# A fused Flamingo block on one core: the QKV products are scheduled two slots earlier, and the splitting of a weight moves between ScalarE, GpSimd and VectorE

## What is computed

```python
ln_out = _ln(hidden_states, ln_w, ln_b)
q  = _ln(_fp8_linear_pertensor(ln_out, wq, wq_scale, q_in_scale).reshape(b, s, g, hpg, d), qln_w, qln_b)
k  = _ln(_fp8_linear_pertensor(ln_out, wk, ...), kln_w, kln_b)
v  = _fp8_linear_pertensor(ln_out, wv, ...)
core = _gqa(q, k, v)                      # softmax(q k / sqrt(d)) v
qx = _ln(_fp8_linear_pertensor(ln_out, wqx, ...), qxln_w, qxln_b)
kx, vx = jnp.split(jnp.einsum('bsi,oi->bso', cond, w_kv_x), 2, axis=-1)
xout = _gqa(qx, _ln(kx, kxln_w, kxln_b), vx)
catq = _div_clamp_fp8(jnp.concatenate([core, xout], axis=-1), proj_smooth)
x = x + jnp.tanh(g_xattn[0]) * jnp.einsum('bsi,oi->bso', catq, wproj) * (proj_in_scale * proj_w_scale)
...
h = bitlinear(_layernorm(x), w_gate_up)   # ternary weights, activations quantized per row
a, b = jnp.split(h, 2, axis=-1)
x = x + jnp.tanh(g_ffn[0]) * bitlinear(jax.nn.silu(a) * b, w_down)
```

## Time and profile before

| | |
|---|---|
| median of 3 runs | 1846.1 us (1844.93 to 1848.54) |
| the profiled execution | 1844.93 us, its span 1843.1 us |
| granted TensorE clock, mean over the span | 0.965 |
| PE, DVE, ACT, POOL busy | 88%, 84%, 74%, 60% of the span |

### The profile page before, as it was taken

How to read it: one execution, slowest core, us unless ns; L and a number is a source line. 1 busy time by engine, 2 the same in 40 slices (tenths; PEclk the granted TensorE clock), 3 DMA queues, 4 the chain that set the end, 5 groups by cost and what they waited for, 6 DMA issues and landing times.

```text
span 1843.1 us, 35164 instructions
## 1 busy us (share of the span) xinstructions
PE 1625.3 (88%) x11147; PEld 1007.0 (55%) x11164; DVE 1543.7 (84%) x3419; ACT 1358.0 (74%) x3383; POOL 1099.5 (60%) x1421
## 2 busy tenths in 40 slices
PE   1368888788999999999999888999999978999995
PEld 1355555455666665666666555666666524444442
DVE  7568899999897899988788999999988857777774
ACT  6468999778989998999997788989988842222222
POOL 3577888777786787888676667767777620000000
PEclk8689999989999999999999999999999989999997
DMA  3257889779999999999898988999998976322200
GB/s 102 95 147 168 183 194 209 167 163 205 226 247 192 206 236 193 207 227 252 187 220 178 224 192 202 233 219 225 226 223 172 206 180 207 92 74 77 69 18 17
DMA packets 669596, 325.48 MB, mean 177 GB/s; under 512 B 552288, under 2 KB 595424, under 8 KB 669152
## 3 DMA queue, kind: packets, MB, share of 16 engines
q1 hardware_dynamic: 669408, 323.17, 78.1%
HBM read 140.61 MB, written 48.23 MB: 102 GB/s over the span
## 4 chain that ended last, share of the span: by engine, by line
PE 43%; DVE 26%; ACT 11%; POOL 8%; issue 7%; DMA 4%; SPq 1%; ACTq 0%; DVEq 0%; POOLq 0%
PE psum L699 8%; PE psum L654 7%; PE psum L687 7%; PE psum L741 6%; PE psum L716 6%; DVE pp L981 5%; DVE nmx L971 5%; PE psum L661 3%; PE psum L758 3%; DMA pt<-pp 3%; ACT pp L1321 2%; PE psum L674 2%; ACT psum L1310 2%; DVE xh L954 1%; ACT raw L1241 1%
## 5 line engine op out<-in xcount | busy, mean ns | idle before, releaser
L687 PE MATMUL psum<-qk 128*128 128x512 f16 x1536 | 423.3, 385 | 28.6 <-DVE pp L981 22.5
L699 PE MATMUL psum<-pt,vv 128*128 128x512 f16 x1536 | 398.7, 383 | 37.2 <-ACT cy L1329 22.0
L654 PE MATMUL psum<-wbt,xqt 128*128 128x256 f16 (+1 forms) x4096 | 406.7, 249 | 15.9 <-DVE xqt L898 11.4
L1310 ACT ACTIVATE psum<-psum,nmx 128x512 f32<-128x512 f32 x512 | 349.1, 682 | 76.6 <-DVE nmx L971 75.4
L654 PEld LDWEIGHTS psum<-wbt,xqt 128*128 128x128 f16 x4096 | 329.5, 99 | 125.4 <-DVE xqt L898 11.6
L981 DVE SCALAR_TENSOR_TENSOR pp<-psum,prs,pp 128x512 f16<-128x512 f32 x512 | 379.3, 741 | 2.6 <-ACT pp L1321 2.4
L971 DVE TENSOR_REDUCE nmx<-psum 128x1 f32<-128x512 f32 x512 | 345.5, 675 | 30.7 <-PE psum L687 30.0
L1321 ACT ACTIVATE pp<-psum,prs 128x512 f16<-128x512 f32 x512 | 361.7, 706 | 6.1 <-DMA pt<-pp 5.7
L699 PEld LDWEIGHTS psum<-pt,vv 128*128 128x128 f16 x1536 | 147.4, 98 | 234.5 <-issue 47.4
L1564 POOL TENSOR_TENSOR qk<-y,qk 128x512 f16<-128x512 f32 x192 | 232.7, 1212 | 16.0
L687 PEld LDWEIGHTS psum<-qk 128*128 128x128 f16 x1536 | 143.3, 99 | 115.6 <-DVE pp L981 28.1
(11 more groups left out here) (176 smaller groups left out, 2773.0 us busy)
## 6 DMA issues: line engine op xcount, KB each, us to landing
wbt<-ws SPq DMA_DIRECT2D x192, 256.0 KB, 3.8
ws<-wbt SPq DMA_DIRECT2D x64, 256.0 KB, 4.0
catd<-cy SPq DMA_DIRECT2D x64, 256.0 KB, 3.4
raw<-in_wgu SPq DMA_DIRECT2D x64, 256.0 KB, 3.6
raw<-in_w SPq DMA_DIRECT2D x32, 384.0 KB, 3.8
wbt<-catd SPq DMA_DIRECT2D x6, 2048.0 KB, 9.9
pt<-pp SPq DMA_TRANSPOSE x512, 3.8
raw<-in_wp SPq DMA_DIRECT2D x32, 256.0 KB, 3.6
```

The lines of the kernel that those rows point to most:

```text
L654: ins = e.matmul(bank[:, o0:o0 + c1 - c0], xv[:, v, kt * 512 + tt * 128:kt * 512 + (tt + 1) * 128], wb[i][:, h, kt, c0:c1], start=kt == 0 ...
L687: ins = e.matmul(SB(n), qk[i][:, jq, u, ss], qk[i][:, jk, w, :], start=k == 0, stop=k == 2)
L699: ins = e.matmul(OB, v[:, t, u, att, :], src[:, w, t, :], start=t == 0 and k == 0, stop=t == 3 and k == 2)
L1310: e.activation(SB(n), SB(n), ACT.Exp, bias=nmx[:, k], accum_out=psm[:, k]).then_inc(s["exp"], 1)
```

## The change

- The QKV products move two slots earlier (GEMM_AT 9 to 7), with what belongs to them: the ramp begins two slots earlier (FIRST), the first weights are loaded earlier, `group_factors`, the stores of the split weights and the loads for the end move, and the reload of stored weights (`load_w`) comes one slot earlier. Part 0 now falls on t = 2, part 1 on t = 3, part 2 on t = 0, part 3 on t = 1.
- PVS becomes 1, 1, 2 and 0 units; the first head transpose of a group moves from t = 1 to t = 0.
- The four `x_turn` move by one or two slots; `scale_whole` moves one slot earlier and `weight_scales` too; `ctx_hi` and `ctx_lo` ("parts") move two slots earlier.
- A split changes engines: POOL makes the float16 copy (slot m), DVE the subtraction (slot m+1). ACT keeps the sum.
- For group 1 the first product waits for all six weight tiles, not for four.

```diff
-FIRST, PAST = -26, NSLOT + 20
+FIRST, PAST = -28, NSLOT + 20
 PVLAG = 9
-PVS = ((0,), (1, 2), (3,), ())
-GEMM_AT = 9
+PVS = ((0,), (1,), (2, 3), ())
+GEMM_AT = 7
-HEADS_AT = (10, 12, 14, 16, 18, 22)
-FACTORS_AT = 6
+HEADS_AT = (9, 12, 14, 16, 18, 22)
+FACTORS_AT = 4
-RAMP_LOAD = (-27, -26, -25, -20, -20, -19)
-W0_AT = -22
+RAMP_LOAD = (-29, -28, -27, -22, -20, -19)
+W0_AT = -24
-STORE_W = 10
+STORE_W = 8
-WG_AT, CAT_AT, X2_AT = (444, 490), (474, 498), 507
+WG_AT, CAT_AT, X2_AT = (444, 488), (472, 496), 506
-SCALE_AT = {"sum": 303, "whole": 308, "fac": 309}
+SCALE_AT = {"sum": 303, "whole": 307, "fac": 308}
-    "turn": (19, 24, 35, 51),
+    "turn": (20, 26, 36, 52),
-    "parts": (104, 104, 104, 104),
+    "parts": (102, 102, 102, 102),
...
-                nw, j = divmod(n + 7 + 2 * SLOTS, SLOTS)
+                nw, j = divmod(n + 8 + 2 * SLOTS, SLOTS)
...
-                            q.wait_ge("w_dn", it * 6 + (6 if it > 1 else 4))
+                            q.wait_ge("w_dn", it * 6 + (6 if it else 4))
...
# DVE, job(m), a split:
+                    q.wait_ge("l_hi", JV["l_hi", m])
+                    if stored is not None:
+                        q.wait_ge(f"l_st{i}", JV[f"l_st{i}", stored])
+                        q.wait_ge("l_ab", JV["l_ab", summed])
+                    e.tensor_tensor(o.bitcast(F16)[:, 0:512], f, wps[:, j, :], ALU.subtract).then_inc(s["l_lo"], 1)
...
# ACT:
-            def job_hi(m):
-                j, i = JOBS[m][2], (K0 + m) % 2
-                q.wait_ge(f"raw_ld{i}", JV[f"raw_ld{i}", K0 + m])
-                e.activation(wps[:, j, :], raw[i][:, 0:512], ACT.Copy).then_inc(s["l_hi"], 1)
...
# POOL, job(m), a split:
-                    e.tensor_tensor(o.bitcast(F16)[:, 0:512], f, wps[:, j, :], ALU.subtract).then_inc(s["l_lo"], 1)
+                    q.wait_ge(f"raw_ld{i}", JV[f"raw_ld{i}", K0 + m])
+                    e.tensor_scalar(wps[:, j, :], raw[i][:, 0:512], 1.0, 1.0, ALU.mult, ALU.mult).then_inc(s["l_hi"], 1)
...
-                if JOB_AT.get(n - 1, -1) >= 0:
-                    job(JOB_AT[n - 1])
+                if JOB_AT.get(n, -1) >= 0:
+                    job(JOB_AT[n])
```

More of the change, by code:

```diff
@@ L998, in job @@
             def job(m):
-                if JOBS[m][0] != "tern":
+                what, src, j, _ = JOBS[m]
+                i = (K0 + m) % 2
+                f, o = raw[i][:, 0:512], raw[i][:, 512:768]
+                if what in ("sum", "scale"):
                     return
-                i = (K0 + m) % 2
-                f, ob = raw[i][:, 0:512], raw[i][:, 512:768].bitcast(BF16)[:, 0:512]
                 stored, summed = JB[m]
-                q.wait_ge("l_t1", JV["l_t1", m])
-                q.wait_ge(f"l_st{i}", JV[f"l_st{i}", stored])
-                q.wait_ge("l_ab", JV["l_ab", summed])
-                q.done(e.tensor_scalar(ob, f, MAGIC, 1.0, ALU.subtract, ALU.min))
-                e.tensor_scalar(ob, ob, -1.0, None, ALU.max).then_inc(s["l_t2"], 1)
+                if what == "tern":
+                    ob = o.bitcast(BF16)[:, 0:512]
+                    q.wait_ge("l_t1", JV["l_t1", m])
+                    q.wait_ge(f"l_st{i}", JV[f"l_st{i}", stored])
+                    q.wait_ge("l_ab", JV["l_ab", summed])
+                    q.done(e.tensor_scalar(ob, f, MAGIC, 1.0, ALU.subtract, ALU.min))
+                    e.tensor_scalar(ob, ob, -1.0, None, ALU.max).then_inc(s["l_t2"], 1)
+                else:
+                    q.wait_ge("l_hi", JV["l_hi", m])
+                    if stored is not None:
+                        q.wait_ge(f"l_st{i}", JV[f"l_st{i}", stored])
+                        q.wait_ge("l_ab", JV["l_ab", summed])
+                    e.tensor_tensor(o.bitcast(F16)[:, 0:512], f, wps[:, j, :], ALU.subtract).then_inc(s["l_lo"], 1)
             def weight_sums():
@@ L1416, in act_program @@
                     ctx_hi(b, kt)
-                if JOB_AT.get(n, -1) >= 0 and JOBS[JOB_AT[n]][0] == "split":
-                    job_hi(JOB_AT[n])
                 for at in (n, n - 2):
@@ L1580, in job @@
                 i = (K0 + m) % 2
-                f, o = raw[i][:, 0:512], raw[i][:, 512:768]
                 if what == "split":
-                    stored, summed = JB[m]
-                    q.wait_ge("l_hi", JV["l_hi", m])
-                    if stored is not None:
-                        q.wait_ge(f"l_st{i}", JV[f"l_st{i}", stored])
-                        q.wait_ge("l_ab", JV["l_ab", summed])
-                    e.tensor_tensor(o.bitcast(F16)[:, 0:512], f, wps[:, j, :], ALU.subtract).then_inc(s["l_lo"], 1)
+                    q.wait_ge(f"raw_ld{i}", JV[f"raw_ld{i}", K0 + m])
+                    e.tensor_scalar(wps[:, j, :], raw[i][:, 0:512], 1.0, 1.0, ALU.mult, ALU.mult).then_inc(s["l_hi"], 1)
             q.wait_ge("pre_v", 1)
```

## The result

| | before | after |
|---|---|---|
| median | 1845.0 us (1843.05 to 1848.54) | 1863.4 us (1856.64 to 1868.18) |
| ratio, 95% interval | | 1.0092 [1.0077, 1.0107] |
| profiled execution, its span | 1844.9, 1843.1 us | 1860.7, 1858.9 us |

A forecast was written before the change was run, and what follows sets the result against it. DVE and ACT handing over in each slot were taken to bound slots 0 to 368, PE slots 368 to 488; terms -2 + 3 - 3 - 5 + 4 + 0 - 2 = -5 us gave 1840 profiled, 1841 median, range 1828 to 1857.

The forecast's parts named there:

- What bounds the kernel: Whole kernel: PE bounds slots 440 to 488 and the stretch ahead; DVE and ACT set the pace in 0 to 368.
- The splits: Slots 96 to 304: DVE gains 32 subtractions of 0.85 us, a quarter felt; +4 us, bounds -6 and +30.
- the splits make DVE the bound: Rival, DVE in slots 93 to 306: splits cost +25 us in place of +4, giving 1862 us; chance 0.12.
- PE's four slots: PE's work spread more evenly, longest slot 3.25 to 3.05 us, `stats_a` waits less: -2 us, between -9.6 and +5.
- the new company: DVE's and ACT's four slots, 96 to 368: same work, other instructions sharing a slot; +3 us, between -5 and +15.
- the new company hurts: Rival: ACT's longer slot t = 2 is not made up, +15 us in place of +3, giving 1853 us; chance 0.13.
- The x transposes: Two slots between head and x transpose would end 8.1 us of waits in slots 0 to 96: -3, between -8 and +6.
- no change: Rival: the removed stalls were of an engine that was ahead, so 1846 us, within 0.2%; chance 0.27.
- scale_whole: Slot 308: PE's 3.16 us stall and some 3.2 of slow clock go, 1.5 is new: -5 us, bounds -7 and +1.
- The ramp: Ahead of slot 0: two slots longer but the same weight chain, PE idle there anyway; 0 us, between -1 and +3.
- The end: Slots 486 and 487 lose their products, 1.7 us of PE work moved ahead: -2 us, bounds -3 and 0.
- The signs that I had named as wrong: Slots 96 to 304 over 550 us; DVE split over 1.2 or waiting 10 us; ACT's waits moved; slot 0 over 3 us later.

The follow-up runs named there:

- e2: Kernel before with only the splits changed (POOL copies, DVE subtracts one slot later, ACT sums): 1854.8 us, ratio 1.0041.
- e1: The whole change but with the splits left as in the kernel before: 1846.8 us, ratio 1.0012 to before.
- e8: e1 with ACT's `norm_b` written one slot later, at t = 3 instead of t = 2: 1891.7 us, ratio 1.0242 to before.
- e14: e1 with the products one slot earlier than before instead of two (GEMM_AT 8), and what belongs to them: 1944.3 us, ratio 1.0541 to before.
- e6: Kernel before with only PVS changed to 1, 1, 2, 0 units: 1839.6 us, ratio 0.9964.
- e15: e1 with ACT's four context copies in slot 103 instead of 102: 1843.5 us, ratio 0.9990 to before.
- e16: The whole changed kernel with the context copies in slot 103 instead of 102: 1861.6 us, ratio 1.0077 to before.
- e10: e1 with the first head transpose back in slot 10 and the x transposes in slots 19, 24, 35, 52: 1848.4 us, ratio 1.0013 to before.
- e9: e1 with the output chain behind ACT's copy (clip, subtraction, DVE's steps, store) two slots later: 1864.2 us, ratio 1.0085 to before.
- e3: Kernel before with only `scale_whole` and `weight_scales` one slot earlier and the last x transpose at slot 52: 1842.5 us, ratio 0.9987.
- e4: Kernel before with only the splits' subtraction moved from POOL to DVE, ACT still copying: 1848.8 us, ratio 1.0019.
- e5: e2 with DVE's subtraction replaced by a shorter instruction with one SBUF input that writes zeros: 1850.9 us, ratio 1.0021 to before.

## Why the prediction was wrong, term by term

- **What bounds the kernel.** Right: DVE and ACT handing over in each slot set slots 96 to 304, and PE's stretches hardly moved (-0.3 and -1.3 us). Its boundaries were 2 to 3 us late (the stretch is 543.5 us long, not 546), which changes no term by more than that.
- **The splits: +4 predicted, +12.7 measured in e2.** The rival "the splits make DVE the bound" had +25. This is the first step that failed, and it is one of size: the duration on DVE was 1.08 us in the mean (34.65 busy for 32; 0.98 in e2), not 0.85, and not a quarter of it was felt but two fifths (12.7 of e2's 31.5 us). I named the wait for POOL and its 2.09 us example and gave it no term; it is 9.3 us in 11 waits and breeds the block behind it. Felt per split were 0.4 us (12.7 / 32), near the 0.5 at which I had let the rival decide. My -3 for ACT and POOL was not seen: ACT's 10 us less of work turned into waiting for DVE (39.0).
- **PE's four slots -2 and the new company +3: together +1, measured +11.4 in e1**, which for the stretch holds both, with the moved heads, x transposes and context copies. This is the second failed step, and what is seen of it fits the rival "the new company hurts": t = 2 became the longest slot (2.94 us for 2.64) and t = 3 grew too (2.64 for 2.39), while t = 0 and t = 1 gave back only 0.34 together. So the surplus that I let be made up by the next slot was not made up. Half a line of the term was right: L940 no longer waits. But I valued company by adding up lists for each slot; e8 and e14 show how little such a list can tell: one instruction pair a slot later costs 16 us, all products a slot off 57. In e8 what the list leaves out is seen, when a bank comes free; what it is in e1 stays open.
- **PVS** was predicted inside those -2. Alone it is worth 6.6 us (e6).
- **The context copies** ("parts", 104 to 102) had no term. At the two places where they stand, e15 gives back under 1 us and e16 2.4.
- **The x transposes: -3 predicted, no gain found in e10**, which takes back the distance but not the whole wait. The waits vanished as predicted, L626 is down from the earlier trace rows to the line below; the rival "no change" had said that these were stalls of an engine that was ahead. The same PE gained waits of 7.8 us for heads behind x and 6.3 for weights in slots 0 to 96. That stretch did gain 4 to 5 us, by something that e10 leaves in place and e9 undoes; what it is stays open. A candidate that the prediction didn't name: PE's largest wait there, 12.4 us for POOL at L600, is down to 2.0 after and 1.8 in e10. Its lines before and after stand first; no run tests it.

```profile
PE psum L600 <- POOL spread L1467: 12.4, 5, 4.7
PE psum L600 <- POOL spread L1469: 2.0, 4, 0.9
PE psum L626 <- ACT y L1312: 1.4, 2, 0.7
PE psum L674 <- ACT xqt L1240: 7.8, 4, 3.5
PE psum L654 <- POOL wbt L1513: 6.3, 2, 3.5
```

- **scale_whole: -5 predicted, -4.8 in slots 304 to 320** (e3 against the profiled execution of before), wait and clock window both gone: right in mechanism. The size is partly luck, since it was read from the execution against which it is measured; against e2, e4, e5 and e6 it is 1 to 2.5 us. The new wait of x for DVE's `weight_scales` is 2.3 us after, above the 1.5 that I had put in the sum.
- **The ramp 0:** slot 0 starts at 113.9 for 113.3: right. **The end -2:** slots 440 to 511 are 0.8 us shorter and the part behind them 0.9 longer: nothing gained.
- **The signs that I had named as wrong** came true in part: the stretch is over 550 us, and the waiting for POOL is nearly 10 us. ACT's waits didn't move to its `norm_b` and output copy (they are at L1325 and L1319, the scaling and the exponential); it is PE that waits longer for the output copy. I put 1862 on one rival and 1853 on another. The result lies at the 1862 by luck: the splits alone gave 1855 (e2), and the rest came from the other rival. In the stretch it is half of the one's price (12.7 of 25) and three quarters of the other's (11.4 of 15), a case to which I gave no chance of its own.

## What to carry to other kernels

In a hand-written pipeline the cost of an instruction is not its length alone: before moving one, list which bank or buffer the next user then waits for (44 waits and 31.4 us in e8). A long wait is not yet a cost: look whether the slots around it got longer (around PE's 3.99 us at slot 104 twelve slots took 34.5 us, against 34.2 before). A stall's price read from one execution can hold a stretch of low clock that other executions don't have. Moving work to an engine with idle time is not free if the idle time is waiting inside a chain: price the new wait and the blocked length too, and be wary of letting POOL produce what DVE takes up at once with two inputs in SBUF, since POOL's next instruction can start first. Two slow rivals that don't exclude each other need a case in which both come.

## What the runs showed of the hardware

When DVE's subtraction of two SBUF tiles meets an instruction of POOL's on 512 columns that got in first, it ends 0.54 to 0.55 us behind the end of POOL's, in all 43 cases of after, e2 and e4: 1.63 us begun 0.07 or 0.12 us behind a subtraction of POOL's of 1.15 to 1.20, 1.03 to 1.09 behind its short copy, 0.89 to 1.42 in between, 0.68 undisturbed. When DVE is first, POOL's subtraction takes 1.62 for 1.20. Who is first is decided by less than 0.1 us, and the starts in the trace don't tell it to the last: once in after DVE began 0.02 us behind POOL, took 0.68 all the same, and POOL's took 1.71. Beside POOL's instructions on 2 or 4 columns DVE took 0.68 to 0.69. The form with one SBUF input was not free of it (e5): 0.41 us beside nothing, 0.83 begun 0.07 us behind POOL's short copy, 1.37 begun 0.12 us behind POOL's subtraction, each ending 0.28 to 0.29 behind POOL's end.

The granted clock does not answer the same stall in the same way each time. Behind a stall of PE of 3.16 us it was 0.51 for 7 us before; behind one of 3.17 in e5 it stayed at 1.00, behind 3.16 in e2 it was 0.76, that is, at the lower level for a part of the 7 us. The slots 304 to 320 took 48.05, 44.35 and 45.73 us, and 43.25 without the stall (e3).
